# Two PSUM banks for the transposed scores and one for everything else, with the feed-forward products in slots of their own

## The reference

```python
scores = einsum('bhqd,bhkd->bhqk', Q, K) / sqrt(D)         # Q, K, V: x @ W.T + b, split in 16 heads
thresh = top_k(scores, U)[0][..., -1:]                     # the 31st largest score of each row
scores = where(scores < thresh, -inf, scores)
context = einsum('bhqk,bhkd->bhqd', softmax(scores), V)
x = layernorm(x + context @ Wo.T + bo)
gate, up = x @ wg.T, x @ wu.T                              # int weights scaled by 1/127, hidden width 768
x = layernorm(x + (silu(gate) * up) @ wd.T)
```

## Time and profile before

| | PE | DVE | ACT | POOL |
|---|---|---|---|---|
| busy, us | 2733.1 | 2502.0 | 2496.6 | 2401.5 |
| share of the span of 3080.8 us | 89% | 81% | 81% | 78% |

### The profile page before, as it was taken

The page is one execution under the profiler, slowest core; times in us unless marked ns, Lnnn a source line. Parts: engine busy times, 40 slices in busy tenths (PEclk is TensorE's granted clock), DMA queues, the critical chain, the costliest instruction groups (busy, mean ns, idle before and its releaser), DMA issues.

```text
span 3080.8 us, 81076 instructions
## 1 busy us (share of the span) xinstructions
PE 2733.1 (89%) x21030; PEld 1498.6 (49%) x21375; DVE 2502.0 (81%) x12298; ACT 2496.6 (81%) x5894; POOL 2401.5 (78%) x1677
## 2 busy tenths in 40 slices
PE   5988989899998998889989998988989998998986
PEld 2444545455454454544545454444545545454554
DVE  4888888888888878888888888878888888888851
ACT  4888888888889877788888888878878887898852
POOL 1888887788788877788788787877878787788881
PEclk7899999999999999999999999999999999999987
DMA  2201011110111101011010111102111010111000
GB/s 85 48 20 44 22 50 29 28 44 24 38 27 40 38 22 42 19 43 36 25 45 25 37 29 36 39 20 47 25 35 37 25 44 26 36 30 32 20 16 7
DMA packets 91143, 102.64 MB, mean 33 GB/s; under 512 B 34513, under 2 KB 52946, under 8 KB 90578
## 3 DMA queue, kind: packets, MB, share of 16 engines
q1 hardware_dynamic: 88544, 93.73, 12.7%
q10 hardware_dynamic: 2034, 2.76, 0.3%
HBM read 20.86 MB, written 8.39 MB: 9 GB/s over the span
## 4 chain that ended last, share of the span: by engine, by line
PE 51%; ACT 19%; issue 14%; DVE 12%; SPq 1%; POOL 1%; ACTq 1%; DVEq 1%; DMA 0%; POOLq 0%
ACT above L479 8%; PE bench L681 6%; PE Y_ps L617 6%; PE ST_ps L628 6%; PE bench L687 6%; PE ST_ps L631 6%; PE ctxT_ps L645 5%; ACT junk L469 5%; DVE cand L877 5%; PE bench L558 4%; PE Y_ps L615 4%; ACT PT L487 3%; PE Y_ps L614 3%; PE bench L674 2%; PE bench L589 2%
## 5 line engine op out<-in xcount | busy, mean ns | idle before, releaser
L1109 POOL TENSOR_SCALAR mask<-S,thr,mb 128x512 bf16<-128x512 f32 x1024 | 2114.0, 2077 | 42.9 <-POOL mb L1103 34.6
L877 DVE MAX8 cand<-Y_ps 128x8 f32<-128x128 f32 x4096 | 1075.5, 283 | 6.7 <-issue 6.7
L870 DVE TENSOR_SCALAR_CACHE_REDUCE S<-S_ps,na 128x512 f32<-128x512 f32 x1024 | 758.1, 740 | 298.7 <-PE S_ps L604 240.7
L469 ACT ACTIVATE junk<-S,at_zero,slope 128x512 bf16<-128x512 f32 x1024 | 824.8, 805 | 96.5 <-DVE S L870 96.5
L479 ACT ACTIVATE above<-S,s,steep 128x512 bf16<-128x512 f32 x1024 | 825.1, 806 | 0.6
L487 ACT ACTIVATE PT<-ST_ps 128x512 f32<-128x512 f32 x1024 | 596.9, 583 | 224.2 <-PE ST_ps L631 222.9
L628 PE MATMUL ST_ps<-QS,KS 64*128 64x512 f32 x1024 | 457.3, 447 | 122.2 <-ACT PT L487 117.0
L604 PE MATMUL S_ps<-KS,QS 64*128 64x512 f32 x1024 | 523.5, 512 | 4.2 <-DVE S L870 2.8
L617 PE MATMUL Y_ps<-KS,QS 64*128 64x512 f32 x1024 | 523.1, 511 | 1.0 <-issue 0.7
L615 PE MATMUL Y_ps<-above,nbig 128*128 128x512 bf16 x1020 | 399.0, 391 | 74.9 <-DVE cand L877 49.6
L631 PE MATMUL ST_ps<-nbig,mask 128*128 128x128 bf16 x4096 | 417.9, 226 | 0.0
(11 more groups left out here) (125 smaller groups left out, 3681.5 us busy)
## 6 DMA issues: line engine op xcount, KB each, us to landing
QS<-Qhi SPq DMA_DIRECT2D x512, 32.0 KB, 2.0
KS<-Khi SPq DMA_DIRECT2D x512, 32.0 KB, 2.0
KS<-Klo SPq DMA_DIRECT2D x512, 32.0 KB, 2.0
QS<-Qlo SPq DMA_DIRECT2D x512, 32.0 KB, 2.0
xTs<-in_xT SPq DMA_DIRECT2D x17, 512.0 KB, 3.8
xs<-in_x SPq DMA_DIRECT2D x16, 512.0 KB, 3.9
out<-xs SPq DMA_DIRECT2D x16, 512.0 KB, 2.9
hT<-in_wgT ACTq DMA_DIRECT2D x1, 768.0 KB
```

Of the source, the lines that this page charges most:

```text
L469: nc.scalar.activation(junk[:, :], S[:, score_place(j)[0], :], ACT.Tanh, bias=at_zero[:, :], scale=slope[:, hb, col:col + 1], accum_out=s0 ...
L870: nc.vector.tensor_scalar(S[:, at, :], S_ps[n % 2][:, :], na[:, hb, col:col + 1], None, ALU.add, op1=ALU.max, accum_out=rmax[:, n % RING:n ...
L877: mx = nc.vector.max(cand[:, j % CANDS, i, :], Y_ps[j % 2][:, i * BW:(i + 1) * BW])
L1109: nc.gpsimd.tensor_scalar(mask[:, h % MASKS, t, :], S[:, score_place(j)[0], :], thr[:, r:r + 1], mb[:, r:r + 1], ALU.is_lt, op1=ALU.add).t ...
```

## The change

It takes one bank from the bench and gives it to the transposed scores, orders the uses so that there is at most one product in a slot, gives `th` two places, and puts three kinds of bench reads on VectorE ahead of the evacuation.

```diff
-HALF_USES = {4: "v", 11: "q", 12: "k", 13: "keys", 14: "gram", 15: "quad", 17: "sums",
-             26: "v", 33: "q", 34: "k", 35: "keys", 36: "gram", 37: "quad", 56: "sums"}
+HALF_USES = {4: "v", 10: "q", 12: "k", 14: "keys", 17: "gram", 19: "quad", 21: "sums",
+             26: "v", 33: "q", 34: "k", 35: "keys", 36: "gram", 37: "quad", 55: "sums"}
-CTX_T, OUT_PROJ, X1_T = (27, 28), (30, 31), (38, 39)
-FFN_SLOTS = {43: 0, 45: 1, 47: 2, 50: 3, 52: 4, 54: 5}
+CTX_T, OUT_PROJ, X1_T = (28, 29), (30, 31), (38, 39)
+GATE_SLOTS = {42: 0, 44: 1, 46: 2, 49: 3, 51: 4, 53: 5}
+UP_SLOTS = {43: 0, 45: 1, 47: 2, 50: 3, 52: 4, 54: 5}
...
-        ST_ps = ps("ST_ps", [P, L])
+        ST_ps = [ps(f"ST_ps{i}", [P, L]) for i in range(2)]
-        bench = [ps(f"bench{i}", [P, L]) for i in range(2)]
+        bench = ps("bench", [P, L])
-        ready = [sem(f"ready{i}") for i in range(2)]
-        taken = [sem(f"taken{i}") for i in range(2)]
+        ready = sem("ready")
+        taken = sem("taken")
-        th = sb("th", [P, L])
+        th = sb("th", [P, 2, L])
...
             # exponentials (ScalarE)
-                nc.scalar.activation(PT[:, j % 4, :], ST_ps[:, :], ACT.Exp, scale=SCALE).then_inc(exp_done, 1)
+                nc.scalar.activation(PT[:, j % 4, :], ST_ps[j % 2][:, :], ACT.Exp, scale=SCALE).then_inc(exp_done, 1)
...
                         if what == "gate":
-                            act.wait_ge(ready[k], use + 1)
+                            act.wait_ge(ready, use + 1)
+                            if part > 1:
+                                act.wait_ge(h_done, (b - 1) * NF + part - 1)
+                            nc.scalar.activation(th[:, part % 2, :], bench[:, :], ACT.Tanh, scale=0.5 * DEQ).then_inc(th_done, 1)
+                        if what == "up":
+                            act.wait_ge(ready, use + 1)
                             if part:
                                 act.wait_ge(h_done, (b - 1) * NF + part)
-                            nc.scalar.activation(th[:, :], bench[k][:, :], ACT.Tanh, scale=0.5 * DEQ).then_inc(th_done, 1)
...
             # turned (TensorE)
-                if not (first and n == TURNED):
-                    pe.wait_ge(exp_done, T - TURNED)
+                ST = ST_ps[j % 2]
+                if not (first and n < TURNED + 2):
+                    pe.wait_ge(exp_done, T - TURNED - 1)
...
             # on_bench (TensorE): ahead of every product
-                    k, use = place(b, n, what, part, first, rest)
-                    pe.wait_ge(taken[k], use)
+                    use = place(b, n, what, part, first, rest)
+                    pe.wait_ge(taken, use)
```

More of the change, by code:

```diff
@@ L114, in uses_of @@
             uses.append(("x1_t", X1_T.index(n)))
-        if n in FFN_SLOTS:
-            uses += [("gate", FFN_SLOTS[n]), ("up", FFN_SLOTS[n])]
+        if n in GATE_SLOTS:
+            uses.append(("gate", GATE_SLOTS[n]))
+        if n in UP_SLOTS:
+            uses.append(("up", UP_SLOTS[n]))
         if n in DOWN_SLOTS:
@@ L128, with count @@
 TURN_OF, ACT_TURN_OF = 5, 7
[L130 to L138, removed]
+def count(first, rest, upto=(TILES, None)):
+    have = 0
     for n in range(TILES):
@@ L142, in counts @@
                 return have
-            have[BANKS[n, use]] += 1
+            have += 1
     return have
-PROLOGUE_COUNT = [len(PROLOGUE[0::2]), len(PROLOGUE[1::2])]
-FIRST_COUNT = counts(True, False)
-BATCH_COUNT = counts(False, False)
+FIRST_COUNT = count(True, False)
+BATCH_COUNT = count(False, False)
 def place(b, n, what, part, first, rest):
-    k = BANKS[n, (what, part)]
-    have = counts(first, rest, (n, (what, part)))[k]
+    have = count(first, rest, (n, (what, part)))
     if first:
[L157 to L162, removed]
+        return len(PROLOGUE) + have
+    return (b - 1) * BATCH_COUNT + (len(PROLOGUE) + FIRST_COUNT + have)
 def build(nc, xT, x, wqT, wkT, wvT, woT, bq, bk, bv, bo, wgT, wuT, wdT, ident_in, blocks_in, heads_in, ranks_in, out):
@@ L238, in build @@
         x1T = [sb(f"x1T{i}", [P, C, L], F32R) for i in range(2)]
-        th = sb("th", [P, L])
+        th = sb("th", [P, 2, L])
         ups = sb("ups", [P, L])
+        brow = th[0:1, 0, 0:DM]
+        bparts = [ups[0:1, i * (DM // 2):(i + 1) * (DM // 2)].bitcast(BF16) for i in range(3)]
         hT = sb("hT", [P, NF, L])
@@ L829, in moments, with head_gram, quadratic_terms @@
-            def moments(part, at):
+                dve.nop(nofuse=True).then_inc(taken, 1)
+            def head_gram(use):
+                dve.wait_ge(ready, use + 1)
+                nc.vector.tensor_tensor(gram[:, :], bench[:, 0:P], blk[:, :], ALU.mult).then_inc(taken, 1)
+            def quadratic_terms(use):
+                dve.wait_ge(ready, use + 1)
+                nc.vector.tensor_tensor(quad[:, :], bench[:, :], hi[0][:, :].bitcast(F32),
+                                        ALU.mult).then_inc(taken, 1)
@@ new lines, in slots @@
+                        if what == "out_proj":
+                            if part == 0:
+                                dve.wait_ge(x_loaded, b * 16)
+                            residual((2 * part, 2 * part + 1), use)
+                        if what == "x1_t":
+                            dve.wait_ge(x1T_copied, b * 2 - 1 + part)
+                            to = [x1T[j][:, :, part * 2 * P:(part + 1) * 2 * P].rearrange("p c (n t) -> p n c t", n=2)
+                                  for j in range(2)]
+                            nc.vector.tensor_tensor(to[1], bench[:, :].rearrange("p (n c t) -> p n c t", n=2, c=C),
+                                                    to[0].bitcast(F32), ALU.subtract).then_inc(taken, 1)
@@ L1031, in slots @@
+                        if what == "down":
+                            residual((part,), use)
                         if what == "turn":
-                            normalise((n - 1 - GROUP) // 16 % NG, b * NG + n // 16 - 1, (k, use))
+                            normalise((n - 1 - GROUP) // 16 % NG, b * NG + n // 16 - 1, use)
                     for part in range(3):
@@ L1139, in slots @@
                     for what, part in uses_of(n - 1, first, rest) if n else []:
-                        if what == "gate":
-                            k, use = place(b, n - 1, "gate", part, first, rest)
-                            pool.wait_ge(taken[k], use + 1)
                         if what == "up":
-                            k, use = place(b, n - 1, "up", part, first, rest)
-                            pool.wait_ge(taken[k], use + 1)
-                            nc.gpsimd.tensor_tensor(hT[:, part, :], th[:, :], ups[:, :], ALU.mult).then_inc(h_done, 1)
+                            use = place(b, n - 1, "up", part, first, rest)
+                            pool.wait_ge(taken, use + 1)
+                            nc.gpsimd.tensor_tensor(hT[:, part, :], th[:, part % 2, :], ups[:, :], ALU.mult).then_inc(h_done, 1)
                     if not rest and HALF_USES.get(n - 4) == "sums":
```

298 lines of the change are left out of this document (124 added, 174 removed).

## The result

The changed kernel takes 3118.97 us (median of 4 runs, 3115.72 to 3121.99), the kernel before 3085.69 us (4 runs, 3081.59 to 3086.96). The ratio is 1.011 with an interval of 1.0092 to 1.0128. It is slower by 33 us, where 32 us less was forecast, and it lies outside the range. Of the prediction's cases the nearest is the first rival, that the single bench bank decides (3136).

What follows compares the result with a forecast made beforehand. TensorE was taken as nearest to the bound, no engine full. Per batch 4.6 + 1.2 - 2.8 = 3.0 us gained, -45 us in 15 batches, +15 for the ends, gave 3052.6, as median 3054 us; range 2985 to 3108.

Steps and rivals of the forecast that it cites:

- the first rival: Handovers in slots 26, 34, 42 to 47, 56, 58 cost 7.1 us per batch; about 3136 us, slower, chance 0.24.
- second bank of transposed scores: TensorE's waits before transposed scores, 7.5 us in batch 7, nearly all go; gain of 4.6 us per batch.
- new order of uses: Spreading products helps slots 11 to 20, moments hurt in 22 to 25; gain of 1.2 us per batch.
- single bench bank: Each bench product waits until the one before is read; handovers cost 2.8 us per batch.
- ends, once: Prologue and last feed-forward part lose 15 us once, between 8 and 28.
- The discount at k: Slot 34, k behind q: wait of 1.25 us taken as 0.6, since VectorE's residual now runs ahead of it.
- the upper end of 28: Ends cost 28 us if the last part runs TensorE at its lower clock, about 1 us on some twelve products.
- The ring: Last feed-forward part: one bank makes gate and up take 4.30 us instead of 2.83; six parts cost 8.8 us.
- VectorE's early reads cost nothing: Reads ahead of the evacuation are free where VectorE idles; in slot 40 the evacuation starts up to 0.7 us later.
- its own signs: Score waits under 30 us, bench waits 30 to 60, gate and up every 4.3, TensorE's busy time within 20.
- the slower case: The first rival, chance 0.24; its sign was waits ahead of bench products exceeding 75 us over the run.
- the wait only moves: TensorE's score waits move behind VectorE's maxima or sign counts, past 180 us at the maxima; 3086 us, chance 0.14.

Runs made afterwards that it cites:

- one bank each: Changed kernel with one bank for the transposed scores and one for the bench, a bank staying unused: 3180.29 us, ratio 1.0308.
- order alone: Changed kernel's order, slots and early reads, with the banks of before (one for transposed scores, two for the bench): 3066.67 us, ratio 0.9905 to the kernel before.
- the banks alone: Changed kernel's banks, gate and up in own slots, but old places of q to sums and transposed context, bench reads behind the evacuation: 3189.98 us, ratio 1.0305.
- the reads put back: Changed kernel with the VectorE reads of out_proj, x1_t and down back behind the evacuation: 3180.19 us, ratio 1.0284.

## Why the prediction was wrong

The sum had four terms. In the same units, with what the runs showed, per batch:

| | forecast | measured | from |
|---|---|---|---|
| second bank of transposed scores | -4.6 | -3.7 | one bank each against changed |
| new order of uses | -1.2 | -0.9 | order alone against before |
| single bench bank | +2.8 | +5.3 | one bank each against order alone |
| sum | -3.0 | +0.7 | 185.61 - 184.94 |
| ends, once | +15 | +27 | table of the parts of the span |

The three measured terms are steps of one path (before, order alone, one bank each, changed), so they add up by construction.

- *Step that failed: "What the single bench bank adds", 2.8 us per batch.* The mechanism was named and its price was half of the real one; it makes 2.5 x 15 = 38 of the 69 us by which the span missed; the ends make 12, the second bank of scores 13, the order 4, and batch 0 the rest. I priced the handovers by today's distance between product and read, and took discounts on them. Measured waits of the changed kernel per batch, without the recomputed thresholds: first down product 2.3 (forecast 0.85), second x1 behind the first 1.6, flags 1.0 and v in slot 26 0.4 (0.4 for these three together), q behind the turned context 0.6 (none), first x1 0.5, mostly behind the normalised rows (none), keys 0.5 (none), gate in 42 0.45 (0.3), k 0.7 (0.6), ups 0.1 (0.6). That is 8.3 in all against 2.8, and the path above prices the missing bank at 5.3. The discount at k, for the residual that no longer stands in the way, was right: in slot 34 of batch 7 the wait is 0.63 us, as shown above. The missed price is at the first down product, at x1's pair and at the handovers that got no price of their own. The read ahead of the down product ends 1470.26 + 0.42 - 1468.33 = 2.35 us after the scores of slot 58 in the kernel before, and 1480.85 + 0.42 - 1477.02 = 4.25 us after them now, since the moments of the second half come one slot earlier: 1.9 us (1.7 as a mean of batches 2 to 13), where I had added next to nothing. Two kernels with late reads bear this out, which differ in the order alone: with the banks alone, sums in 56, no wait of the down products (L697) behind the turned context is among the named ones (24.9 us idle, 21.5 of it behind the residual), and with the reads put back, sums in 55, it is 34.6 us.
- x1's pair was missed since I looked for handovers between uses of different kinds one slot apart. Products of the same kind in consecutive slots hand over too, and here through two engines in a row.
- *The ends, 15 us.* Named step by step, with the lower clock as the upper end of 28 and the value taken without it. The ring itself was nearly right, 10.1 us against 8.8. It came at the lower clock on top, and this 8.7 us had been taken at nothing. The row of before showed the products at 1.10 to 1.20 us, but the granted clock was at the lower level there too until 3043.3 us and rose in mid-ring; in the changed kernel it stayed low from 3048.8 to 3100.0. Nothing in that row said that it would rise when the ring stretched from 2.83 to 4.3 us with the same 2.3 us of products in it. The prologue cost 4.9 instead of 3.2: the wait of k is 3.07 us as forecast, and the first product of the prologue started 1.2 us later (14.90 against 13.66), ahead of any handover.
- *The second bank of scores.* Right in that these waits go (122.2 to 5.6 us), and wrong in what they are worth. The step was that a wait in front of TensorE is a gain in full where TensorE is the bound. With one bench bank the waits taken away came back at the bench and behind the maxima (20.0 us per batch with and without the second bank), and the 3.7 us that were kept are busy time, which the sum didn't have: the score product alone became shorter by 2.6 us per batch against the kernel before. That 3.7 is near 4.6 is luck to that extent.
- *The new order.* Right in size, -0.9 against -1.2. Of its two sides, the kernel before with sums in 21 shows the moments' waits: they move from 17 to 21 into 22 to 26 and stay as large. What I didn't see is that a third place, slot 27, has the gain without the loss.
- *That VectorE's early reads cost nothing* held, and was too modest. With one bench bank they are worth 54 us.
- The rival "The bench bank decides" had 7.1 us of handovers, near the 8.3 measured, but partly by luck: its 2.0 at slot 58 was right, its 2.1 for the ups was not (0.1), its 1.25 at k was the price without the relief, and x1's pair wasn't among its parts.
- The same rival said that the change is slower once the handovers cost over 4.8 us per batch. They cost 5.3. The rule of the Trainium skill that was weighed there ("Perfetto Trace Analysis", section "Matmuls": rotate independent groups through banks) agrees with this case, where 5.3 us per batch are lost on the group that stopped rotating and 3.7 won on the one that began to. The rule doesn't say which group to give a bank to.

By its own signs: the waits of the transposed scores fell under 30 us (right); bench waits exceeded 75 us by far (the slower case); gate and up in the last part came every 6.25 us and not every 4.3 (wrong); TensorE's busy time fell by 20.5 us, at the edge of the 20. Waits behind the maxima are 132 us, under 180, but this sign was too coarse: without the recomputed thresholds they rose by 24 us, so the rival "the wait only moves" was right in part.

What stays open: the 0.5% of the kernel before with sums in 21; why TensorE's busy time falls by more than the shorter products; and whether the pair of x1 alone can be mended on one bench bank, which wasn't tried.

## What to carry to other kernels

A buffer's worth is in the handovers that it covers. Before taking a bank away, list every pair of neighbouring uses, those of one kind too, with all readers of the first, and price each by the reader's own queue on its worst pass; before giving one, ask where the wait will come back (here 6.6 us of waits per batch went and 6.6 came, with 3.7 us kept as busy time; 3.3 us of spaced handovers kept 2.0). Set single long waits apart before a total is divided by the batches: three of them made 2.0 of 10.3 us here. Long work of the vector engine belongs under slots in which TensorE has extra products, and moving it by six slots was worth 1.5% here. The ends of a pipeline, where nothing lies between the products, have to be priced by themselves, and there idle banks of the main loop can serve.

## What the runs showed of the hardware

- A ring of product and read at the end of the kernel ran TensorE at the lower of its two clocks (granted clock 0.50 from 3048.8 to 3100.0 us), although it never stood still for more than 1.41 us within it: 2.08 us per product against 1.20 us with unused products put between. The clock had fallen ahead of the ring, in 7.11 us of idle time before the transposed x1, and didn't rise again. In the kernel before the first two pairs too take 1.9 to 2.0 us per product, up to 3043 us, and the later ones 1.10 to 1.20. The Trainium skill says in "Perfetto Trace Analysis", section "Matmul Optimizations", that the matmul engine scales its power with utilization, so that products should come back to back. These rows agree.
- A product that had to wait for its bank is also recorded as longer. In the kernel before, the 232 transposed score products that waited for their bank take 497 ns in the median, the other 792 take 393 ns.
- Moving the sums to 27 went with less of the lower clock, 148 us against 90 in the same 14 batches, beside 2.3 us of waits less per batch. That is no rule: with q, k and keys spaced as well the waits fell by another 1.6 us and the lower clock was 113 us.
